# A decoder layer on one Trainium2 core: the last superblock's softmax and attention mixing done in the first five feed-forward bodies

## What is computed

```
q, k = split into 32 half-heads of 16;  v: 16 heads of 32
att  = softmax(q k^T) per token over half-heads          (32 x 32 per token)
diff = att[:16, :16] - lam * att[16:, 16:]
o    = diff @ v, each head divided by its root mean square, * (1 - LAM_INIT)
x1   = layernorm(x + o @ Wo^T + bo)
r_t  = decay * r_(t-1) + ctx_t^2 over each sequence;  x2 = layernorm(x1 + x1 * r)
h    = relu(x2 @ ternary(W_fc)^T)^2;  out = layernorm(x2 + rmsnorm(h) @ ternary(W_proj)^T)
```

## Time and profile before

| | us |
|---|---|
| median of 3 runs | 1148.79 (1144.92 to 1149.48) |
| the profiled execution's own time | 1146.96 |
| its span from first to last instruction | 1145.1 |
| TensorE busy | 1042.4 (91%) |
| VectorE busy | 932.2 (81%) |
| ScalarE busy | 566.3 (49%) |
| GpSimd busy | 242.7 (21%) |

### The profile page before, as it was taken

One profiled execution on the slowest core, in us unless ns is written; L12 is line 12 of the kernel. 1 busy time (PEld: TensorE's weight loads), 2 busy tenths in 40 slices (PEclk: granted clock), 3 DMA queues, 4 the chain that ended last, 5 costly groups with the idle time before them and its releaser, 6 DMA issues.

```text
span 1145.1 us, 20366 instructions
## 1 busy us (share of the span) xinstructions
PE 1042.4 (91%) x7008; PEld 823.3 (72%) x7008; DVE 932.2 (81%) x1668; ACT 566.3 (49%) x866; POOL 242.7 (21%) x237
## 2 busy tenths in 40 slices
PE   6999999999999997545898999999999999999994
PEld 5777666667667775434687888888888888888883
DVE  4579898888989999997677896987979969798555
ACT  5342424243333342411656566566665766656672
POOL 5312433425252525052122002020020100200000
PEclk9999999999999998666999999999999999999998
DMA  7887686959696867897041410413014112110010
GB/s 280 273 202 185 137 247 128 254 124 247 138 239 148 207 149 201 228 235 261 1 110 38 111 38 0 110 37 73 37 37 110 37 55 55 37 38 1 1 37 37
DMA packets 166535, 139.71 MB, mean 122 GB/s; under 512 B 139968, under 2 KB 139968, under 8 KB 160576
## 3 DMA queue, kind: packets, MB, share of 16 engines
q1 hardware_dynamic: 95296, 113.57, 36.1%
q10 hardware_dynamic: 71168, 25.17, 8.8%
HBM read 82.09 MB, written 52.43 MB: 117 GB/s over the span
## 4 chain that ended last, share of the span: by engine, by line
PE 56%; DVE 16%; SPq 8%; ACT 6%; DMA 6%; issue 5%; ACTq 1%; POOL 1%; DVEq 0%; POOLq 0%
PE ps_f L699 19%; PE ps_s L715 17%; PE ps_o L651 6%; PE ps_f L545 6%; PE ps_s L562 3%; SPq L397 3%; SPq L465 3%; DMA w_scr<-w_in 2%; DVE row_sum L1041 2%; DMA w_in<-in_fc_turned 2%; DVE st L1054 1%; DVE xtl L991 1%; DVE o_sb L1076 1%; SPq L367 1%; ACT xth L805 1%
## 5 line engine op out<-in xcount | busy, mean ns | idle before, releaser
L699 PE MATMUL ps_f<-x2h,w 128*128 128x512 f32 x512 | 204.3, 399 | 1.8 <-DVE x2l L1224 1.6
L699 PE MATMUL ps_f<-x2l,w 128*128 128x512 f32 x512 | 200.7, 392 | 0.0
L715 PE MATMUL ps_s<-w,hh 128*128 128x512 f32 x500 | 196.8, 394 | 2.0 <-DVE o_sb L1076 2.0
L715 PE MATMUL ps_s<-w,hl 128*128 128x512 f32 x500 | 195.0, 390 | 0.0
L1232 DVE TENSOR_TENSOR hl<-h_sb,hh 128x512 fp32r<-128x512 f32 x128 | 96.1, 751 | 101.1 <-ACT hh L917 101.0
L545 PE MATMUL ps_f<-xth,wh 128*128 128x512 f32 x376 | 155.4, 413 | 3.9 <-issue 2.1
L545 PE MATMUL ps_f<-xtl,wh 128*128 128x512 f32 x376 | 146.8, 391 | 0.0
L545 PE MATMUL ps_f<-xth,wl 128*128 128x512 f32 x376 | 146.8, 391 | 0.0
L1421 POOL TENSOR_TENSOR xb<-xb,bob 128x512 f32<-128x512 f32 x32 | 49.2, 1569 | 441.8 <-DMA xb<-in_x 441.8
L562 PE MATMUL ps_s<-qbd,k 128*32 128x128 f32 x2048 | 124.8, 411 | 9.3 <-DMA qbd<-q_scr 9.3
L907 ACT ACTIVATE r_sb<-ps_f 128x512 f32<-128x512 f32 x128 | 75.4, 589 | 87.2 <-PE ps_f L699 87.1
(11 more groups left out here) (143 smaller groups left out, 1832.1 us busy)
## 6 DMA issues: line engine op xcount, KB each, us to landing
q_scr<-f_sb ACTq DMA_DIRECT2D x32, 256.0 KB, 4.0
k_scr<-f_sb ACTq DMA_DIRECT2D x32, 256.0 KB, 2.8
w_scr<-w_in SPq DMA_DIRECT2D x16, 512.0 KB, 5.6
k<-k_scr SPq DMA_DIRECT2D x8, 1024.0 KB, 8.2
qbd<-q_scr SPq DMA_DIRECT2D x128, 64.0 KB, 4.2
v_scr<-f_sb ACTq DMA_DIRECT2D x32, 256.0 KB, 5.6
v<-v_scr SPq DMA_DIRECT2D x64, 128.0 KB, 5.5
o_scr<-o_sb SPq DMA_DIRECT2D x8, 1024.0 KB, 5.6
```

The lines of the kernel that those rows point to most:

```text
L699: last = nc.tensor.matmul(ps_f[:, j % 2, :], w1[:, j // 2, k, (j % 2) * P:(j % 2 + 1) * P], xx[:, k, :], start=(k == 0 and xx is x2h), sto ...
L715: last = nc.tensor.matmul(ps_s[:, t, :], a[:, j % 4, t * P:(t + 1) * P], w2[:, j, :], start=(j == 0 and a is hh), stop=(j == HC - 1 and a ...
```

## The change

- In the passage only the turning of superblock 7's scores stays (`late_turn`). Cleaning, maximum and subtraction go to body 0 (`late_clean`, `late_shift`), the second half of the softmax to the starts of bodies 1 and 2 (`late_second`), `late_diff_turn` to body 2, and the four mixings to bodies 2, 3 (twice) and 4 (`LATE_MIX`). `o_scale` and the write of o follow in body 4.
- The difference of superblock 7 goes through HBM (`d_scr`) and comes back as four quarter-size operands `dbd_q`, one after another.
- `out_project`'s operands share one buffer (`otl` lies on `ot`), and the squared context is made and scanned in `cx` itself (`kv` is gone). So `ot_load` waits for `out_project`, and `cx_load` for `scan_transpose`.
- The loads of the passage stand in another order; half of `dbd_load(6)` is issued by ScalarE's queue.
- Phase B's loop is written out.

```
         def phase_b(eng, body):
             body(0, True, False, True)
-            with eng.Fori(1, NSB - 2) as i:
+            for i in range(1, NSB - 2):
                 body(i, True, True, True)
...
+        LATE_CLEAN = {1: 1, 4: 2, 11: 3}
+        LATE_SHIFT = {1: 1, 4: 2, 13: 3}
+        LATE_EXP = {1: 0, 2: 1, 6: 2, 14: 3}
+        LATE_SECOND = {1: (0, 2), 2: (1, 3)}
+        LATE_MIX = {(2, 11): 0, (3, 1): 1, (3, 4): 2, (4, 1): 3}
...
             def body_b(i, prep, fin):
+                if i == 2:
+                    late_spill()
+                    dbd_q_load(0)
+                if i == 3:
+                    dbd_q_load(2)
+                    dbd_q_load(3)
                 if prep:
-                    hold((ot_hi, i + 2), (ot_lo, i + 2), (cx_sq, at(i, TT, 2 * TT)))
-                    load_first(i + 2)
+                    hold((op_ps, at(i, TT, 2 * TT)), (o_wr, at(i, 16, 48)))
+                    ot_load(i + 2)
...
+            def late_mix(i, c):
+                pe.wait_ge(dbd_q_ld, 128 * (c + 1))
+                if c == 0:
+                    pe.wait_ge(v2_ld, at(LATE, 128, 128))
+                if c == 0:
+                    pe.wait_ge(z_done, at(i + 1, TT, TT - 1))
+                elif c == 2:
+                    pe.wait_ge(av_cp, at(LATE, 4, 2))
+                else:
+                    pe.wait_ge(m_step, at(i - 1, M_STEPS, 1))
...
+            mix(NSB - 2, 2, 0, G // 4)
             scores(NSB - 1, 2, 0, FULL)
-            mix(NSB - 2, 2, 0, G // 4)
-            scores(NSB - 1, 3, 0, FULL)
             mix(NSB - 2, 3, 0, G // 4)
             for t in range(TT):
                 out_project(0, t)
-            for c in range(4):
-                mix(NSB - 1, c, 0, G // 4)
+            scores(NSB - 1, 3, 0, FULL)
...
+            def late_clean(c):
+                nc.vector.tensor_scalar(late_neg[:], y, 0.0, -FMAX, ALU.min, ALU.max)
+                nc.vector.scalar_tensor_tensor(out=y, in0=y, scalar=0.0, in1=late_neg[:], ...)
+            def late_shift(c):
+                nc.vector.tensor_reduce(out=mx, in_=y, op=ALU.max, axis=AX)
+                nc.vector.tensor_scalar(mx, mx, FMAX, None, ALU.min)
+                nc.vector.scalar_tensor_tensor(out=y, in0=y, scalar=FMAX, in1=mx..., op1=ALU.subtract)
...
```

More of the change, by code:

```diff
@@ new lines, in _ @@
+            ot_load(0)
+            second_half_load(NSB - 1)
+            sp.dma_start(woh[:].bitcast(F32), wo_scr[0]).then_inc(wo_ld, 16)
+            sp.dma_start(wol[:].bitcast(F32), wo_scr[1]).then_inc(wo_ld, 16)
+            sp.dma_start(bob[:], bo.rearrange("(a n) -> a n", a=1).to_broadcast([P, D])).then_inc(bo_ld, 16)
+            sp.dma_start(xb[:], x_t[0]).then_inc(xb_ld, 16)
+            cx_load(0)
+            w_write(NSB - 1, 1)
+            hold((av_ps, at(NSB - 1, 16, 0)), (wt_wr, at(NSB, 32, 0)))
@@ L891, in ctx_square @@
                         act.wait_ge(rs_ps, at(i, TT, 0))
-                nc.scalar.activation(kv[:, k, :], cx[:, k, :], ACT.Square).then_inc(cx_sq, 1)
+                nc.scalar.activation(cx[:, k, :], cx[:, k, :], ACT.Square).then_inc(cx_sq, 1)
             def x2_upper(i, t):
                 act.wait_ge(xx_ps, at(i, TT, t + 1))
+                if t == 0 and not later(i):
+                    for n in range(3):
+                        act.wait_ge(f_wr[n], at(NSB, 64, 0))
+                    act.wait_ge(wt_wr, at(NSB, 32, 0))
                 if t == 0 and later(i):
@@ L1062, in diff_turn, with late_diff_turn @@
+            def late_diff_turn():
+                v.wait_ge(s_diff, at(LATE, 2, 2))
+                for gh in range(2):
+                    last = nc.vector.transpose(
+                        late_dt[:, gh * (G // 2):(gh + 1) * (G // 2), :].rearrange("p (n m) a -> p n m a", m=2),
+                        late[:, gh, :, 0:H].rearrange("p (n m) a -> p n m a", m=2))
+                last.then_inc(d_tr, 1)
             def diff_turn(i):
@@ L1303, in _ @@
                 x2_lower(0, t)
-            out_lower(1)
             def body_b(i, prep, fin, ahead):
+                if not later(i):
+                    late_clean(0)
+                for c in LATE_SECOND.get(i, ()):
+                    late_second(c)
                 for j in range(HC):
@@ L1343, in body_b @@
                             out_lower(i + 2)
+                    if not later(i) and j == 0:
+                        out_lower(1)
+                        late_shift(0)
+                    if not later(i) and j in LATE_CLEAN:
+                        late_clean(LATE_CLEAN[j])
+                    if not later(i) and j in LATE_SHIFT:
+                        late_shift(LATE_SHIFT[j])
+                    if (i, j) == (2, 0):
+                        late_diff_turn()
+                    if (i, j) in LATE_MIX:
+                        mixed_turn(LATE, LATE_MIX[i, j])
+                    if (i, j - 2) in LATE_MIX:
+                        square_sum(LATE, LATE_MIX[i, j - 2])
+                    if (i, j) == (4, 4):
+                        rms_seed(LATE)
                 if prep:
@@ L1431, in body_b @@
                         add_bias(i + 1, t)
-                if not later(i):
-                    o_scale(NSB - 1)
+                if i == 2:
+                    pool.wait_ge(d_tr, LATE + 1)
+                    pool.wait_ge(d_wr, 16)
+                    nc.gpsimd.memset(dbd_q[:], 0.0).then_inc(zeroed, 1)
+                if i == 4:
+                    o_scale(LATE)
             phase_b(pool, body_b)
```

248 lines of the change are left out of this document (170 added, 78 removed).

## The result

| | before | after |
|---|---|---|
| median of 15 runs each | 1149.36 us | 1142.25 us |
| all runs | 1144.92 to 1153.74 | 1139.5 to 1144.98 |
| ratio, with its 95% interval | | 0.9939 [0.9923, 0.9954] |
| the profiled execution's own time | 1146.96 | 1143.45 |
| mean granted TensorE clock | 0.964 | 0.963 |

The change makes the kernel faster by 0.6%, where 1.5% was forecast; 1142 lies inside the range. The passage gave what was forecast. The feed-forward bodies took back two thirds of it.

A forecast was written before the change was run, and what follows sets the result against it. It took TensorE as the bound nearly everywhere, VectorE in the passage, body 0 between. Passage, body 0, mixings and waits in bodies 1 to 4: 1146.96 - 20 - 3 + 4.2 + 3.3 = 1131.5, said as 1131 us; range 1120 to 1144.

The forecast's parts named there:

- The passage, -20: Passage: with VectorE's moved work gone, the first up comes 20 us earlier, at 516 to 517.
- the forecast's chain: Passage: wol lands at 475.7, out_project(0) ends at 489.6, last scores and turning follow, x1_norm at 493, first up 23 later.
- Body 0, -3: Body 0: removed and added VectorE work give 84 us against 87.0, 3 us saved.
- VectorE's own sum: Body 0: VectorE works 65.4 - 6.9 + 20.3 = 79 us, with one forced pause of 3 to 4 us.
- The step-by-step reading of the forecast: Body 0: second and third out_project wait for add_projection behind two cleanings and two shifts, 3.5 us each; the rest catches up.
- The forecast's upper end for this body, 98: Body 0: upper bound of 98 us, the old 12.6 of waits again on top, +11.
- Bodies 1 to 4, +7.5 with the mixings: Bodies 1 to 4: four mixings add 4.2 us on TensorE, and waits behind moved VectorE work add 3.3 us.
- a term put at nothing: Body 4: GpSimd's clearing of dbd_q and its o_scale fall into its idle time, with no cost counted.
- The loop written out, 0: Phase B's loop: at most 2.2 us to gain, taken as 0; the gap ends with VectorE's x2l, not a branch.
- the loads end last: Rival, passage: second ot_load held up behind w2, so w1 and the context land later; +13, 1144 us; chance 0.10.
- body 0 loses its clock: Rival, body 0: TensorE stands in nearly every step and its granted clock halves; some 25 us, 1156 us; chance 0.08.
- No difference: Rival: the passage gains 10 and body 0 gives it back with the mixings; 1147 us; chance 0.04.

The follow-up runs named there:

- xb_early: The changed kernel with the loads of bob and the first xb issued on SyncE ahead of the second half of qbd; 1141.92 us, ratio 0.9944.
- before_bias: The kernel before, with GpSimd's add_bias made to wait for the first x2_lower in every body from 1 on, loop kept; 1142.93 us, ratio 0.9943.
- best1: The changed kernel with block 1's split operands made in the passage, add_bias of block 2 and GpSimd's last four multiplies made to wait; 1131.07 us, ratio 0.9842.
- best3: best1 with GpSimd's add_bias made to wait for the first x2_lower in every body; 1132.63 us, ratio 0.9851.
- scale_later: The changed kernel with GpSimd's last four multiplies made to wait until body 5 has begun instead of running in body 4; 1144.27 us, ratio 0.9954.
- before_straight: The kernel before, with only the loop over five feed-forward bodies (and SyncE's loop) written out; 1148.74 us, ratio 0.9998.

## Why the prediction was wrong

**The passage, -20: right, 20.7, in part by luck.** `out_project(0)` waited for `wol` as forecast. Its start was 3.7 us sooner after the first `dbd` issue than in the forecast's chain (21.1 for 24.8): `wol` was issued 2.2 us sooner and landed in 7.0 us, not 8.8. Behind it the path was not the forecast's, which went over TensorE to the last scores and their turning. The scores ended at 489.8, and `x1_norm` stood behind VectorE's own chain: from 481.85 to 494.31, without a pause, VectorE added the four projections, scanned and turned, 12.5 us of which the forecast's chain had only the turning. This chain began 3.4 us late, waiting for `add_bias`. So `x1_norm` came 19.5 us behind the start of `out_project`, not 17.3, and from there to the first `up` it took 25.2 us and not 23, the 2 us being tiny operations of `x1_norm` beside GpSimd. The early start and the two longer stretches nearly cancel. `xb_early` shows besides that the loads set this time together, not `wol` alone.

**Body 0, -3: wrong, +4.0. This is the largest miss, 7 us.** The failed step is to take the body's length from "VectorE's own sum": VectorE's busy time, 79 us, and a few pauses. VectorE was busy 73.7 us, fewer than the sum, in a body of 91. The sum was too large because `hl`, the scans and `otl` took 5.1 us less than before; GpSimd was busy 23.1 us in this body before and 12.4 after, and that this is the reason is likely but not shown. And VectorE was never full; it was late three times in its order. The step-by-step reading of the forecast had the wait ahead of the second `out_project`, which came out at 1.3 us, smaller than the 3.74 of the earlier trace rows. It did not have the other two, 2.8 us for the split operands and 6.4 us for `x2l`. The `x2l` wait was there before, 3.38 us long, and more than half of that was `add_bias` (`before_bias`: 1.46 without it). A wait that exists already should have been the first candidate to grow by the work put ahead of it; the sum spoke only of the longest one.

In TensorE's idle time, 1.95 us ahead of `down(0, 0)` and 2.4 ahead of the second `out_project` went away, and 2.8 and 3.0 came: it grew from 9.3 to 10.5 us, where the forecast let it fall. The other 2.8 us are matmuls at a lower granted clock, 0.91 for 0.96. Most of them lie behind the wait for `x2l`: from there to the end of the body the same 33 matmul records take 9.15 us at a granted clock of 0.70, and before the change 6.59 at 1.00. How much of this clock comes with the waits stays open, since `best1` and `best3` differ by as much with equal waits. The forecast's upper end for this body, 98, doesn't follow from its words either: 12.6 on top of 84 or 87 is 96.6 or 99.6.

**Bodies 1 to 4, +7.5 with the mixings, measured +11.1, and body 5 -0.8.** Bodies 2 and 3 came as forecast in sum, +5.9 for 6.0: the three mixings added 4.0 us to TensorE's busy time, 1.3 each and not 1.06, and its waits grew by 1.9 us, not 2.8. `late_second` cost nothing in body 1. The failed step is "GpSimd's clearing of `dbd_q` and its `o_scale` in body 4 fall into its idle time", a term put at nothing. It is true of GpSimd, and the wrong question. The multiplies lay beside VectorE's `x1_norm`: body 4 was 80.5, and without them 75.9 (`scale_later`), so they cost about 4.6 us. The forecast had cited the contention one paragraph below and applied it to body 0 alone.

**The loop written out, 0: nearly right.** 2 us by `before_straight`, within the 2.2 of the forecast, and the observation behind it (the gap ends with `x2l`, not with a branch) held: `before_bias` closes the same gap in the hardware loop. In bodies 1 and 5 of the changed kernel it is closed too, which is their -0.7 and -0.8; what closed it there isn't shown, since the loop written out gives only 0.4 of it. The Trainium skill, "Runtime: NRT & Kernel Launch", Instruction fetch mechanics, says that a taken branch out of the fetched window stalls for its page. By it the gap would be the loop's; at most 0.15 us a body of such a stall is in these traces.

**The rivals.** Nothing of "the loads end last" came. Of "body 0 loses its clock" 2.8 us came, not 25. "No difference" had the right shape, a gain given back in body 0 and with the mixings, with the wrong sizes. Two of the forecast's own signs of being wrong showed: body 0 over 88 us, and more than 3 us of waits in body 4 (3.5).

In sum: -20.7 for -20, +4.0 for -3, +10.4 for +7.5 in bodies 1 to 5.

## What to carry to other kernels

When work moves from a stretch where its engine is the bound to one where it has room, busy time says only that it fits. What it costs is read from the operation behind it on its engine for which another engine waits, and the first place to look is a wait that is already there. An operation placed in GpSimd's idle time must be checked against what VectorE does in these microseconds: of the 18 us that `best1` gains, seven come from moving two GpSimd passes by a few us without touching the work itself. And compare versions by the lengths of their stages and the waits in them, since medians that scatter by 3 us hide effects which the length of a steady body shows to 0.1. A body whose clock varies, as body 0 here, is read by its waits.

## What the runs showed of the hardware

- VectorE beside a GpSimd multiply or add of 1.25 us each, by form: two inputs from SBUF (`hl`, `h_acc`) 0.68 to 1.78 us; one with an input from PSUM (`xb<-ps_t,xb`, `x2l<-ps_t,x2h`) 0.68 unchanged; `BATCH_NORM_STATS2` 0.69 and `TENSOR_REDUCE` 1.21 unchanged; `TENSOR_SCALAR` 128x512 0.43 to 0.81, and a tiny one 0.18 to 1.22; four scans, which take 2.6 us, 5.8. The Trainium skill, "SBUF — State Buffer", Who interferes with whom, says that VectorE contends with two SBUF inputs or in its two-port modes and otherwise not; the trace agrees in every form listed. An operation of 0.16 us takes 1.2 us then, about the length of the GpSimd operation that it meets.
- GpSimd pays as well: four multiplies took 5.04 us beside the tiny chain and 8.24 beside large operations.
- After TensorE's wait at the end of body 0 the same four transposes took 0.63 us in some profiles and 1.09 in others, at waits of equal length (3.23 us in `best1`, 3.19 in `best3`). What decides between them isn't shown.
